# A state-space mixer with mixture-of-experts on one core: z and output projections as three split products, and a new order of every engine's work

## What is computed

```python
xn = x * rsqrt(mean(x * x) + EPS) * norm_w
zxbcdt = einsum("bld,ed->ble", xn, in_proj_w)      # z 1024, xBC 1280, dt 16 columns
conv = sum(pad[:, k:k + l, :] * conv_w[:, k] for k in range(4)) + conv_b
xBC = conv * sigmoid(conv)                          # x 1024, B 128, C 128
dt = softplus(dt + dt_bias)
y = ssd(x * dt, dt * A, B, C)                       # chunks of 128 tokens, a state is carried
y = (y + D * x) * (z * sigmoid(z))
y = y * rsqrt(mean(y * y) + EPS) * gnorm_w
out = x + einsum("bld,ed->ble", y, out_proj_w)
```

## Time and profile before

| | us |
|---|---|
| median of 3 runs (5838.91 to 5846.02) | 5845.8 |
| the profiled execution | 5848.4 |
| its span, first to last instruction | 5846.6 |
| TensorE busy in the span | 5613.9 (96%) |
| VectorE busy | 3597.2 (62%) |
| GpSimd busy | 3535.2 (60%) |
| ScalarE busy | 2627.2 (45%) |

### The profile page before, as it was taken

One profiled execution on the slowest core, in us unless ns is written; L12 is line 12 of the kernel. 1 busy time (PEld: TensorE's weight loads), 2 busy tenths in 40 slices (PEclk: granted clock), 3 DMA queues, 4 the chain that ended last, 5 costly groups with the idle time before them and its releaser, 6 DMA issues.

```text
span 5846.6 us, 109797 instructions
## 1 busy us (share of the span) xinstructions
PE 5613.9 (96%) x28797; PEld 4286.0 (73%) x28798; DVE 3597.2 (62%) x10033; ACT 2627.2 (45%) x5588; POOL 3535.2 (60%) x2980
## 2 busy tenths in 40 slices
PE   5999999999999999994999999999999999999999
PEld 3666666666666666663888888887888888888887
DVE  4889888888898898883444444443444444444454
ACT  3555555555555555551333333333333333333322
POOL 2667667667676676673555555554555555555587
PEclk8999999999999999996999999999999999999999
DMA  5443444444444444343688788778678778878687
GB/s 203 163 149 144 162 155 152 154 143 163 158 145 165 147 146 160 145 151 133 138 225 222 183 202 224 164 177 238 138 182 203 160 161 218 208 199 201 132 277 248
DMA packets 340193, 1028.38 MB, mean 176 GB/s; under 512 B 57109, under 2 KB 61461, under 8 KB 339173
## 3 DMA queue, kind: packets, MB, share of 16 engines
q1 hardware_dynamic: 194232, 703.53, 32.9%
q0 software_dynamic: 145568, 321.56, 28.1%
q10 hardware_dynamic: 144, 0.29, 0.0%
HBM read 580.45 MB, written 444.74 MB: 175 GB/s over the span
## 4 chain that ended last, share of the span: by engine, by line
PE 52%; DMA 1%; POOL 0%; issue 0%; DVE 0%; SPq 0%; ACT 0%; POOLq 0%; ACTq 0%
PE bank L1244 45%; PE bank L1379 4%; PE bank L1386 2%; PE bank L1573 0%; PE bank L1582 0%; DMA w_lo<-lo_dram 0%; POOL acc_c L1555 0%; DMA h_c<-h_dram 0%; DMA lst_i<-list_dram,row 0%; DMA xg_e<-h_dram,ids 0%; POOL o_c L1559 0%; POOL acc_c L1546 0%; DMA acc_dram<-y_e,ids 0%; POOL lst_i L1172 0%; SPq L1531 0%
## 5 line engine op out<-in xcount | busy, mean ns | idle before, releaser
L1360 POOL DMA_INDIRECT acc_dram<-y_e,ids x576 | 910.4, 1580 | 1113.1 <-ACT y_e L1432 789.1
L1244 PE MATMUL bank<-w_hi,x_hi 128*128 (+1 forms) x2560 | 1056.1, 413 | 1.7 <-DVE x_lo L1647 1.2
L1244 PE MATMUL bank<-w_hi,x_lo 128*128 (+1 forms) x2560 | 1000.8, 391 | 0.0
L1244 PE MATMUL bank<-w_lo,x_hi 128*128 (+1 forms) x2560 | 1000.7, 391 | 0.0
L1450 DVE TENSOR_TENSOR h_lo<-bank,h_hi 128x256 fp32r<-128x256 f32 x576 | 243.8, 423 | 763.9 <-ACT h_hi L1421 763.7
L1432 ACT ACTIVATE y_e<-bank,xg_e 128x512 f32<-128x512 f32 x576 | 396.4, 688 | 698.4 <-PE bank L1244 698.4
L645 POOL DMA_INDIRECT list_dram<-tok_id,pos x512 | 594.9, 1162 | 156.0 <-issue 154.8
L1352 POOL DMA_INDIRECT xg_e<-h_dram,ids x576 | 571.0, 991 | 193.9 <-issue 174.9
L1426 ACT ACTIVATE th_f<-bank 128x256 f32<-128x256 f32 x576 | 221.3, 384 | 1011.2 <-PE bank L1244 1011.2
L811 PEld LDWEIGHTS bank<-xn_t,w_in 128*128 128x128 f32 x5120 | 587.8, 190 | 67.0 <-ACT btok L687 65.4
L811 PE MATMUL bank<-xn_t,w_in 128*128 128x131 f32 x5120 | 605.4, 276 | 14.8 <-ACT btok L687 14.1
(11 more groups left out here) (247 smaller groups left out, 10448.6 us busy)
## 6 DMA issues: line engine op xcount, KB each, us to landing
hi_dram<-w_hi_m SPq DMA_DIRECT2D x130, 768.0 KB, 3.3
lo_dram<-w_raw SPq DMA_DIRECT2D x130, 768.0 KB, 4.8
w_hi<-hi_dram SPq DMA_DIRECT2D x130, 768.0 KB, 7.4
w_lo<-lo_dram SPq DMA_DIRECT2D x130, 768.0 KB, 10.2
w_raw<-in_w_experts_dram SPq DMA_DIRECT2D x128, 768.0 KB, 5.0
acc_dram<-zeros SPq DMA_DIRECT2D x130, 256.0 KB, 2.8
acc_c<-acc_dram SPq DMA_DIRECT2D x128, 256.0 KB, 3.5
h_dram<-h SPq DMA_DIRECT2D x64, 288.0 KB, 4.1
```

Of the source, the lines that this page charges most:

```text
L1244: last = nc.tensor.matmul(acc, a, b, start=(i == 0), stop=(i == len(terms) - 1))
L1360: pool.indirect_dma_start(acc_dram[r % NACC], bass.IndirectOffsetOnAxis(ap=ids[:, r:r + 1], axis=0), y[:, r % YSLOTS, :], None, compute_op ...
```

## The change

z and the output projection use `split_products`: the weights are split in the setup (`wz_hi`, `wz_lo`, `wo_hi`, `wo_lo`), the inputs in each chunk (`xn_hi` by ScalarE, `xn_lo` by VectorE; `y_hi` by ScalarE, `y_lo` by VectorE). The output projection runs in two parts: the 16 products on y_hi, and 8 on y_lo, with the transposes of xr(e) between them. The three taps stay on VectorE. The order of the step is new on every engine, and x1 with its statistics moves to the head of the next step (as chunk t). gz and xbc have one buffer instead of two, the state is updated in place, y_hi and y_lo lie over x2s and x1s, the masked C·B block gets a tile of its own in SBUF (`cbm`), and the modulation rows come in three tiles that are reloaded apart.

```diff
-        w_in = sb("w_in", [P, KD, DIN])
-        w_out = sb("w_out", [P, KI, DM])
+        w_in = sb("w_in", [P, KD, XBC + NH])
+        wz_hi = sb("wz_hi", [P, KD, DI], FP32R)
+        wz_lo = sb("wz_lo", [P, KD, DI], FP32R)
+        wo_hi = sb("wo_hi", [P, KI, DM], FP32R)
+        wo_lo = sb("wo_lo", [P, KI, DM], FP32R)
...
+                    for k in range(KD):
+                        dve.wait_ge(s_act_set, 5 + k)
+                        nc.vector.scalar_tensor_tensor(out=wz_lo[:, k, :], in0=wz_raw[:, k, :], scalar=norm_w[:, k:k + 1],
+                                                       in1=wz_hi[:, k, :].bitcast(FP32), op0=ALU.mult, op1=ALU.subtract)
...
+                    for k in range(KI):
+                        dve.wait_ge(s_act_set, 5 + KD + k)
+                        nc.vector.scalar_tensor_tensor(out=wo_lo[:, k, :], in0=wo_raw[:, k, :], scalar=gnorm_w[:, k:k + 1],
+                                                       in1=wo_hi[:, k, :].bitcast(FP32), op0=ALU.mult, op1=ALU.subtract)
...
+                    if ws is not None:
+                        split_store(sp, ws, 1)
+                    if t is not None:
+                        sp.wait_ge(S["x1_done"], t + 1)
+                        sp.dma_start(rows_of(x1_dram, t), x1[:, 1 - p, :]).then_inc(x1_st[1 - p], 16)
...
+                        act.wait_ge(S["xnT_sb"], f + 1)
+                        at_least(act, S["z_ps"], 2 * f)
+                        nc.scalar.copy(xn_hi[:], xn_t[:, :, OLD:]).then_inc(S["xn_hi"], 1)
...
+                        nc.scalar.copy(y_hi[:].rearrange("p k t -> p (k t)"), bank[2][:]).then_inc(S["yT_sb"], 1)
...
+                    if f is not None:
+                        pe.wait_ge(S["taps"], XGROUPS * f + 2)
+                        pe.wait_ge(S["xn_lo"], f + 1)
+                        split_products(nc, half(0), [lambda k, t=t: t[:, k, :] for t in (xn_hi, xn_lo)],
+                                       [lambda k, t=t: t[:, k, 0:512] for t in (wz_hi, wz_lo)], KD).then_inc(S["z_ps"], 1)
...
-                        for i in range(KI):
-                            last = nc.tensor.matmul(half(7), y_t[:, i, :], w_out[:, i, :], start=(i == 0), stop=(i == KI - 1))
+                        first = [(y_hi, k, w) for k in range(KI) for w in (wo_hi, wo_lo)]
+                        for i, (a, k, w) in enumerate(first):
+                            nc.tensor.matmul(half(7), a[:, k, :], w[:, k, :], start=(i == 0), stop=False)
...
+                        pe.wait_ge(S["ylo_done"], c + 1)
+                        for k in range(KI):
+                            last = nc.tensor.matmul(half(7), y_lo[:, k, :], wo_hi[:, k, :], start=False, stop=(k == KI - 1))
...
-                    if f is not None:
-
-                        at_least(dve, S["z_ps"], 2 * f)
-                        ts(xn_t[:, :, 0:OLD], xn_t[:, :, P:P + OLD], col(starts, f), None, ALU.mult).then_inc(S["carry"], 1)
...
+                        conv.end()
+                    if e is not None:
+                        at_least(dve, S["z_ps"], 2 * e)
+                        at_least(dve, S["xn_hi"], e)
+                        ts(xn_t[:, :, 0:OLD], xn_t[:, :, P:P + OLD], col(starts, e), None, ALU.mult).then_inc(S["carry"], 1)
...
-                        tt(state[:], tmp_s[:], bank[2][:], ALU.add).then_inc(S["state_done"], 1)
-                        dve.wait_ge(S["yadd_done"], c + 1)
-                        dve.wait_ge(S["gz_done"], 2 * c + 2)
-                        tt(y[:], y[:], gz[:, p, :], ALU.mult).then_inc(S["y_done"], 1)
+                        tt(y[:], y[:], xt[:], ALU.add).then_inc(S["yx_done"], 1)
+                        dve.wait_ge(S["yx_done"], c + 1)
+                        dve.wait_ge(S["gz_done"], 2 * c + 2)
+                        tt(y[:], y[:], gz[:], ALU.mult).then_inc(S["y_done"], 1)
+                        dve.wait_ge(S["states_ps"], c + 1)
+                        dve.wait_ge(S["tmps_done"], c + 1)
+                        tt(state[:], state[:], bank[2][:], ALU.add).then_inc(S["state_done"], 1)
```

More of the change, by code:

```diff
@@ L25 @@
 DIN = 2 * DI + 2 * P + NH
+XBC = DI + 2 * P
 EXPERTS, TOPK, FF = 64, 8, 256
@@ L407, in mixer @@
         etk = sb("etk", [P, NH])
-        x1s = sb("x1s", [P, DI])
-        x2s = sb("x2s", [P, DI])
+        with ExitStack() as until_states:
+            x1s = until_states.enter_context(nc.sbuf_tensor("x1s", [P, DI], FP32))
+            x2s = until_states.enter_context(nc.sbuf_tensor("x2s", [P, DI], FP32))
+        y_lo = sb("y_lo", [P, KI, P], FP32R)
+        y_hi = sb("y_hi", [P, KI, P], FP32R)
         lm = sb("lm", [P, NH * P])
-        tmp_s = sb("tmp_s", [P, DI])
         y = sb("y", [P, DI])
@@ L661, in _, with step @@
             def _(act):
[L662 to L664 removed]
+                def step(d, e, f, c, t, q, r, p, ws):
                     if c is not None:
@@ L790, in transposes @@
-                    def transposes():
+                        at_least(pe, S["ylo_done"], c)
+                        for i in range(2):
+                            last = nc.tensor.matmul(half(6 - i), above[:], lm[:, i * 512:(i + 1) * 512], start=True, stop=True)
+                        last.then_inc(S["rows_ps"], 1)
+                        pe.wait_ge(S["xt_sb"], c + 1)
+                        pe.wait_ge(S["l_in"], 2 * c + 2)
+                        for i in range(2):
+                            at = DI + i * 512
+                            last = nc.tensor.matmul(half(2 + i), above[:], lm[:, at:at + 512], start=True, stop=True)
@@ L856, in step @@
                     if f is not None:
-                        for j in range(2):
-                            pe.wait_ge(S["taps"], XGROUPS * f + 2 - j)
-                            for k in range(KD):
-                                last = nc.tensor.matmul(half(j), xn_t[:, k, OLD:], w_in[:, k, j * 512:(j + 1) * 512],
-                                                        start=(k == 0), stop=(k == KD - 1))
-                            last.then_inc(S["z_ps"], 1)
+                        pe.wait_ge(S["taps"], XGROUPS * f + 1)
+                        pe.wait_ge(S["xn_lo"], f + 1)
+                        split_products(nc, half(1), [lambda k, t=t: t[:, k, :] for t in (xn_hi, xn_lo)],
+                                       [lambda k, t=t: t[:, k, 512:1024] for t in (wz_hi, wz_lo)], KD).then_inc(S["z_ps"], 1)
                     if c is not None:
@@ new lines, in step @@
+                        for k in range(K1, TAPS):
+                            for hf in range(2):
+                                if k == K1:
+                                    dve.wait_ge(S["tap0"], XGROUPS * f + hf + 1)
+                                else:
+                                    conv.wait(2 * (k - K1 - 1) + hf + 1)
+                                for i in group(hf):
+                                    last = stt(out=acc[:, i, :], in0=raw_of(i)[:, k:k + P], scalar=conv_w[:, i, k:k + 1],
+                                               in1=acc[:, i, :], op0=ALU.mult, op1=ALU.add)
+                                if k == TAPS - 1:
+                                    last.then_inc(S["taps"], 1)
+                                else:
+                                    conv.mark(last)
@@ new lines, in step @@
+                    if f is not None:
+                        softplus.begin(f)
+                        dve.wait_ge(S["tap0"], XGROUPS * f + 4)
+                        tt(sp_x[:], half(7)[:, 2 * P:2 * P + NH], dt_bias[:], ALU.add).then_inc(S["dt_raw"], 1)
+                        dve.wait_ge(S["dt_raw"], f + 1)
+                        stt(out=sp_a[:], in0=sp_x[:], scalar=-1.0, in1=sp_x[:], op0=ALU.mult, op1=ALU.max).then_inc(S["dt_abs"], 1)
+                        for k in range(K1, TAPS):
+                            for hf in range(2):
+                                if k == K1:
+                                    dve.wait_ge(S["tap0"], XGROUPS * f + 2 + hf + 1)
+                                else:
+                                    conv.wait(2 * (TAPS - 1 - K1) + 2 * (k - K1 - 1) + hf + 1)
+                                for i in group(2 + hf):
+                                    last = stt(out=acc[:, i, :], in0=raw_of(i)[:, k:k + P], scalar=conv_w[:, i, k:k + 1],
+                                               in1=acc[:, i, :], op0=ALU.mult, op1=ALU.add)
+                                if k == TAPS - 1:
+                                    last.then_inc(S["taps"], 1)
+                                else:
+                                    conv.mark(last)
```

589 lines of the change are left out of this document (318 added, 271 removed).

## The result

The changed kernel takes 6608.1 us (median of 4 runs, 6605.7 to 6614.5) where the kernel before took 5843.8 beside it: a ratio of 1.131, 95% interval 1.129 to 1.133. The profiled execution has a span of 6603.8 us, 757 more than before's 5846.6.

What follows compares the result with a forecast made beforehand. TensorE was taken to bind, overlapping VectorE. Serial work of 48.1 us plus 2.7 for the clock made a 50.8 us chunk against 40.26; over 62 steps, with corrections, 647 onto 5848.4 gave 6495, said as 6500, range 6390 to 6640.

Steps and rivals of the forecast that it cites:

- the clock: TensorE behind its idle stretch: half clock slows y transposes, xbc transposes and projection, costing 2.0 to 3.5 us, taken as 2.7.
- collisions: VectorE's two lm products held by GpSimd through SBUF: possibly 1.1 us a chunk, 68 us in all, left out of the sum.
- The wait that moves: VectorE's carry, now behind the last taps, waits for TensorE's state read, z and chunk states: 8.9 us at least.
- What bound before: Mixer of the old kernel: TensorE binds, VectorE 2.7 us behind, both overlapping in a chunk of 40.26 us.
- The split products: z and output projection as 24 products, 5.45 us each set: each saves 1.45 us; VectorE pays 1.96 a chunk.
- (a): TensorE from the transposes of y to the cumulative-sum products: 10.37 us, less 1.45 for the shorter output projection, 8.92.
- (b): TensorE from the cumulative-sum products through x/B/C, router, diagonal, state read, z and states: 28.09 us.
- (c): VectorE's carry, routing and five 1024-wide products while TensorE idles, with handovers: 11.1 us.
- 48.1: The chunk in us added up around TensorE and VectorE, before any loss to the clock.
- Rival 1: Clock not lost, or back at once: 48.1 us a chunk, 6330 us; chance 0.08.
- Smaller parts: Moved x1, shared buffers, longer GpSimd work, SP's late stores, setup subtractions: costed at nothing, 5 us allowed either side.
- Rival 3: Carry's wait already met, overlap stays, VectorE binds: 39.5 us a chunk, 5800 us; chance 0.04.

Runs made afterwards that it cites:

- e10_z_split_old_order: Kernel before, in its old order, with z alone as three split products: 5900.1 us, ratio 1.009.
- e3_no_idle: Kernel after, with the chunk states computed six times over to fill TensorE's idle stretch: 6696.5 us, ratio 1.146.
- e8_no_idle_pool_early: e3_no_idle with GpSimd's eight list transfers ahead of r2 and the second layer norm's statistics ahead of xg: 6500.7 us, ratio 1.113.
- e7_mod_b_early: Kernel after, with SP loading the rows of mod_b one step earlier, ahead of the weight stores: 6585.0 us, ratio 1.127.
- e1_carry_free: Kernel after, with the carry waiting for the x/B/C products of f and no longer for z: 6101.3 us, ratio 1.045.
- e2_carry_in_before: Kernel before, with only the carry for chunk e moved directly behind the last taps of f, waiting for z: 6537.9 us, ratio 1.119.

## Why the prediction was right

6500 us was forecast, 6390 to 6640; 6608 was measured, in the upper part of the range. The cause was the forecast one. The ordinary chunk came out as added up, in part by luck (see the clock below), and the rest came from two things that the sum did not have: the upper part of the range was meant for the clock behind the idle stretch and for collisions, and something else filled it.

- **The wait that moves.** Right, and shown from both sides: put alone into the kernel before it makes 695 us, taken from the kernel after it gives back 507. VectorE's pause is 10.35 us in an ordinary chunk: 1.07 from the end of the taps to the state read, and 9.28 for state read, z and states, where 1.4 and 8.94 were counted.
- **What bound before.** The prediction read that TensorE binds. e10_z_split_old_order speaks against it: with 1.45 us less of TensorE's work in z a chunk did not become shorter (40.38 us in the quick ones, 40.18 in the kernel before), and TensorE idled more. A loop through both engines set the chunk. The forecast did not suffer, as it followed such a loop.
- **The split products.** Right: state read, z and states take 9.23 us (1588.61 to TensorE's wait at 1597.84), 0.3 more than the 8.94 summed. Products run at 0.23 each. The first one behind fp32 products takes 0.63 to the next (1589.98 to 1590.61), but the fp32 instruction ahead of it only 0.03 in place of 0.43, so the change of type cost nothing here.
- **One chunk.** (a) with the clock: 11.3 measured (1558.22 to 1569.54), 8.92 + 2.7 = 11.6 forecast. (b) 28.3 measured, 28.09 forecast. (c) 11.05 measured, 11.1 forecast. Together 50.67 in this chunk, 50.78 in the mean of the 41, against 50.8.
- **The clock.** Level and place behind the idle stretch were right (y transposes 1.94 as a row, the projection's first products slow), and the size nearly: up to the end of the first projection part 8.24 us in the ordinary chunk against 6.08 in e3_no_idle, 2.2 and not 2.7. What the prediction had wrong is that this loss adds to the chunk. The path through GpSimd's list transfers is nearly as long: in 14 of the 17 chunks of 55 us, where TensorE came earlier, it held the third x/B/C group until 19.73 to 19.75 us behind the y transposes, and the ordinary chunk shown comes there at 20.15. So in the kernel after about 0.4 of the 2.2 us would have come back at full clock (an estimate from these two numbers), and that 50.8 came out is in this term luck. In e3_no_idle a chunk without any half clock takes 51.45 us where TensorE waits on that path, not 48.1. The 48.1 exists (48.5 measured) once that path is shortened too. Rival 1 would therefore not have given 6330. (Of the two idle stretches of over 4 us on which the argument against rival 1 rests, rows 6 show one; the other is the 6.09 us ahead of the h2 transposes at 2653.84.)
- **Left out: a second fall of the clock.** 17 chunks run the diagonal part and the state read at the lower level. Over 50.8 us each they make 77 us. In all 17 TensorE had waited for ScalarE's exponentials before (0.29 us or more); of the 41 ordinary chunks one had such a wait, and its clock did not fall. The wait is not shown to be the cause. In 15 of the 17 the front part had been quicker (first projection part over 6.96 to 7.06 us behind the y transposes, 8.01 to 8.49 in 40 of the 41 ordinary chunks), so TensorE came early to the exponentials; and in e8_no_idle_pool_early the state read is slow without such a wait. What decides it stays open.
- **Left out: the rows of mod_b.** Here a step of the prediction failed: that "SP holds the x1 and weight stores until late in the step" was costed only for those stores, and the reload behind them was not followed. Three chunks lose 43 us over 50.8 each; e7_mod_b_early shows the cause; its time is 23 us shorter.
- **Smaller parts, collisions.** The 77 and 43 us are the gap between 6495 and the result: 6495 + 120 = 6615 against 6608. The first lm product did take longer (2.07 us in place of 1.21, beside a GpSimd product), but 1.07 us of slack were still left behind it, so leaving it out of the sum was right for this kernel. The rule of the Trainium skill that was weighed there ("SBUF — State Buffer", section "SBUF: two separate sides") gives a whole instruction for the lock. e1_carry_free agrees: swb takes 1.26 us in the median in place of 0.23.
- **Rival 3.** Mis-sized: with the wait met at once it forecast 39.5 us a chunk and 5800 us. e1_carry_free measured 44.3 and 6101. Most of the difference are the 3.6 us that routing loses when it no longer waits, which the sum of VectorE's work did not have. Even without the moved wait this order is slower than the old one.

## What to carry to other kernels

Before an instruction is moved in an in-order queue, read what its wait stands for at the new place: a wait for work of the same chunk, on an engine that itself waits for the instructions just ahead, turns two parallel stretches into a serial one, whatever the instruction itself costs. A faster product is worth what lies on the loop that closes a chunk: the same 1.45 us a chunk gained 74 us in the output projection, while split z, with its subtraction on the loop, lost 55. A pause may be hiding other costs, as collisions or a chain on a third engine, so the price of removing it has to be read with those back in place.

## What the runs showed of the hardware that was not expected

- VectorE's small instructions can stand for a whole GpSimd instruction, also those with one tensor as input: sc, a tensor_scalar of 64 columns, took 1.29 us in place of 0.19 in the chunk shown of e1_carry_free, to the end of GpSimd's addition. Reordering GpSimd moved these stands to other instructions and won 18 us in all, the early load of mod_b included.
- The granted clock fell from 1.00 to 0.51 for the diagonal part and the state read in a chunk whose last two idle times were of 0.68 us, and the state read was slow in 17 of the 58 chunks of 49 to 56 us, which run the same instructions. With the 11 us idle stretch filled, it was slow more often, not less (36 of 62 in place of 21). Filling an idle stretch did not keep the clock up for the rest of the chunk.
- Behind an idle stretch of 10.7 us in e2_carry_in_before the clock cost about 1 us, and behind one of 11.05 us in the kernel after 2.2, so stretches of nearly the same length had different prices.
